# New orders for the five engines of a two-layer kernel, from a planner that lets VectorE and GpSimd take turns by instruction, counts TensorE's halved clock behind a rest, and knows some steps in smaller pieces

## The chip, the cores and the metric

The kernel runs on one core of a Trainium2 chip. The metric is the device time of one execution in microseconds (us). The engines of a core are TensorE (PE, matmuls), VectorE (DVE), ScalarE (ACT), GpSimd (POOL) and SyncE (SP, which here issues most of the DMAs); each works through its own program, and semaphores order them against each other.

## The reference

A hidden state of 4 sequences of 1024 tokens with 128 features passes through two layers. Each normalises and adds an attention and a feed-forward part, both read from the same normalised input:

```python
xn = layernorm(x)
x = x + rwkv6_attention(xn) + moe_per_head(xn)      # layer 1
xn = layernorm(x)
x = x + latent_attention(xn) + looped_moe(xn)       # layer 2
```

`rwkv6_attention` mixes each token with the one before it (five mixtures), makes r, k, v, a decay w and a gate, and runs per head (4 heads, 16 keys, 32 values) the recurrence `o = r·(S + u k v)`, `S = exp(w) S + k v`, then a group norm, a gate and a projection. `moe_per_head` projects, cuts every token into 8 heads of 16 features, and gives each head the weighted sum of the 2 best of 16 experts (16 to 64 with an exact gelu, and back). `latent_attention` goes through a latent of 64 features; 16 heads of 8 share one key and value, with causal softmax over 1024 tokens. `looped_moe` does two rounds of RMS norm, router (2 of 8 experts, weights normalised) and a SwiGLU with 256 hidden features, each added to its input.

## The kernel before

**Layers.** After a normalisation the first layer runs until about 527 us of the span and the second until the end, with a barrier between them (`k.meet`): each engine drains its queue and waits for the four others.

**First layer.** `Recurrence` handles the recurrence in 4 turns of two tiles of 512 tokens, by doubling: `LEVELS` 1, 2, 4, ..., 64. At each level h VectorE updates running products (`level`, L1032: the line L1052 for the part before, L1053 for the part behind, L1054 for the totals; this is the step "factors"), and then scales keys and receptances by them (`vector_scales`, four heads of L1131 and one L1136; steps "scale", it, h, n with n = 0, 1, 2 for heads 0 and 1, heads 2 and 3, and L1136). TensorE multiplies the results (L741, "lev"), VectorE and ScalarE place them ("place", L1074). At the end of a turn comes "qk" (the last level and two products), then "carry", "outs" and the group norm: sums of squares (ScalarE L977, TensorE L846), roots (ScalarE L982), L857, L1199 and gate L1203. The expert part goes through 64 units, each with four up products ("up", TensorE L483), four gelus (ScalarE L529), four down products ("down", TensorE L495), the weighting with the router's shares (VectorE L544 to m_prod and m_both, GpSimd L585 adds them, "pair") and a fold ("fold", L508). `Entry` and `Route` prepare already here the routing for the second layer, for four chunks of 512 tokens in the order `MADE`: GpSimd scales a chunk with three instructions L1372, L1374 and L1376 ("scale", c, 1.0 to 1.2 us each), TensorE turns it (L1425, "zn"), VectorE copies it (L1455, "znc"), TensorE makes the logits (L1431, "elog"), VectorE copies these (L1458, "elogc"). At the end TensorE has a fixed filler of eight matmuls (`busy`, L56).

**Second layer.** `Layer1Start` makes the latent (TensorE L1884, "lat"; its input ax_y is copied by ScalarE L1919, "nc"), queries and keys. The attention has 16 tasks: a first pass over scores for the maxima (TensorE L2807, VectorE L2853), a second one for exponentials (TensorE L2952, ScalarE L2976) and the weighted sums (TensorE L2915), then division (VectorE L3043, L3045) and output. `Experts` runs 96 blocks of 128 gathered token slots in 4 phases: rows and weights are fetched by SP (L3167 and L3155), TensorE makes tokens (L3198, "t"), the products a (L3214) and b (L3230), hidden times weights (L3246, "y_half"), ScalarE copies the result and SP stores it; GpSimd's indirect DMAs scatter (L3108) and gather (L3138), and VectorE adds the gathered results ("combine", L3333 and L3338), followed by the last adds (L3054, L3348).

**The order.** The order of all this is not in the code's control flow. Each engine's part of a class is a generator ("stream"), which before each piece of work yields the planned time of that step; `merge(..., ordered=True)` (L64) emits the stream whose time is least. The times come from a planner, `Plan`: steps have a fixed duration (`takes`), a latency to their dependents (`lag`), needs, PSUM banks that they fill and free, and a flag `port` for VectorE and GpSimd steps that exclude each other at SBUF. `FIRST_ORDERS` and `SECOND_ORDERS` hold one string for each engine, one letter for each step; a letter names the stream whose next step comes. `Plan.run(orders)` only replays these strings: it gives each step a time in the given sequence and assigns the PSUM banks in the order of time. So a program depends on the string for the sequence, and on the replayed times for the banks and the interleaving of streams.

## Time and profile before

| | us |
|---|---|
| median of 3 runs | 1273.62 |
| lowest, highest | 1271.74, 1275.04 |
| the profiled execution's own time | 1275.04 |
| its span in the trace | 1273.7 |
| mean granted TensorE clock in it | 0.976 of full speed |
| TensorE / VectorE / ScalarE / GpSimd busy | 1187.4 / 1048.3 / 881.5 / 488.4 |
| instructions | 28619 |

Positions in the trace are microseconds from the start of the span. A busy engine is one with an instruction under way. The profile's page has the busy times, 40 equal slices of the span and the chain of work that ended last; windows give busy times of a stretch with the number of instructions and the granted clock; a timeline gives the instructions of an engine in order, with the idle time in front and the engine, tile and line that ended it in square brackets. "x4" at the end of a timeline row says that four equal instructions stand in one row. Half clock reads 0.50 where a whole window has it.

### The profile page before, as it was taken

What the parts mean: (1) busy time and instruction counts of PE and PEld (TensorE: products, weight loads), DVE (VectorE), ACT (ScalarE), POOL (GpSimd) and SP (SyncE); (2) the same over time, 40 slices, a digit from 0 to 9 for tenths busy, and PEclk for the clock granted to TensorE, in tenths of its full rate; (3) what the DMA queues carried; (4) which work ended last, traced back from release to release, by engine and by line L of the source; (5) the groups of instructions that cost most, each with busy time, mean ns of one, the idle gap of its engine ahead of it and who ended that gap; (6) DMA issues with size and microseconds to landing.
All of it is one profiled execution on the core that took longest, in us unless ns stands there. A gap on an engine that the chain in (4) does not pass through costs nothing.

```text
span 1273.7 us, 28619 instructions
## 1 busy us (share of the span) xinstructions
PE 1187.4 (93%) x11270; PEld 604.5 (47%) x11270; DVE 1048.3 (82%) x1954; ACT 881.5 (69%) x1243; POOL 488.4 (38%) x446
## 2 busy tenths in 40 slices
PE   6889999999998999798999999998999999999977
PEld 3333433334442324465655555555656555555434
DVE  4699779979999885689979898687987898888734
ACT  3588998988798889262366675665766577666666
POOL 3544344374436664420345503555035550000242
PEclk8799999999999999799999999999999999999988
DMA  7433334323232442347654544545434444224111
GB/s 217 131 129 120 108 96 137 101 74 113 94 126 67 142 140 100 99 127 201 191 172 124 172 115 134 163 133 142 109 118 148 119 116 126 76 74 130 32 34 55
DMA packets 129877, 152.97 MB, mean 120 GB/s; under 512 B 16048, under 2 KB 90800, under 8 KB 129616
## 3 DMA queue, kind: packets, MB, share of 16 engines
q1 hardware_dynamic: 111104, 127.50, 33.3%
q0 software_dynamic: 8192, 16.79, 4.6%
q10 hardware_dynamic: 10448, 6.85, 1.8%
q8 instruction: 90, 1.47, 0.5%
q14 instruction: 43, 0.35, 0.1%
HBM read 109.27 MB, written 41.81 MB: 119 GB/s over the span
## 4 chain that ended last, share of the span: by engine, by line
PE 52%; DVE 13%; ACT 4%; issue 3%; DMA 1%; another core or an unknown queue 1%; SPq 0%; DVEq 0%; ACTq 0%
PE ax_sums L2915 9%; PE second_pair L2952 5%; PE second_pair L2807 5%; PE first_pair L495 3%; PE first_pair L483 3%; PE second_pair L3246 2%; PE second_bank L3230 2%; DVE am_top L2853 2%; PE second_bank L3214 2%; ACT ax_prob L2976 2%; PE second_pair L3230 2%; PE second_pair L3214 2%; PE second_bank L3246 2%; PE second_pair L2929 2%; PE second_pair L2825 2%
## 5 line engine op out<-in xcount | busy, mean ns | idle before, releaser
L2976 ACT ACTIVATE ax_prob<-second_pair 128x1024 f32<-128x1024 f32 (+1 forms) x320 | 291.5, 941 | 128.4 <-PE second_pair L2929 64.9
L529 ACT ACTIVATE m_act_h<-first_pair,const 128x1024 f32<-128x1024 f32 x256 | 273.3, 1115 | 47.9 <-PE first_pair L483 39.3
L2853 DVE TENSOR_REDUCE am_top<-second_pair 128x2 f32<-128x1024 f32 (+1 forms) x192 | 222.4, 1175 | 29.0 <-PE second_pair L2807 11.2
L3138 POOL DMA_INDIRECT m_back<-slot_results,mr_slots x128 | 125.5, 980 | 255.4 <-PE second_pair L2952 154.6
L3108 POOL DMA_INDIRECT slot_tokens<-xn,mr_slots x128 | 125.0, 977 | 238.2 <-PE second_pair L3214 104.1
L2915 PE MATMUL ax_sums<-ax_prob,al_vs 128*32 128x512 f32 (+3 forms) x1536 | 155.9, 500 | 5.6 <-ACT ax_prob L2976 4.0
L483 PE MATMUL first_pair<-m_terms,w1s 96*128 96x512 bf16 x512 | 143.5, 387 | 2.7 <-ACT m_act_h L529 2.1
L495 PE MATMUL first_pair<-m_act_h,const 128*32 128x512 f32 x1024 | 129.0, 607 | 7.5 <-DVE m_both L544 2.6
L585 POOL TENSOR_TENSOR m_both<-m_prod,m_both 128x512 f32<-128x512 f32 x64 | 86.2, 1358 | 108.2 <-DVE m_both L544 108.0
L2952 PE MATMUL second_pair<-al_qs,al_ks 51*128 51x512 bf16 (+3 forms) x768 | 113.9, 333 | 10.5 <-ACT ax_prob L2976 4.5
L2807 PE MATMUL second_pair<-al_ks,al_qs 48*128 48x512 bf16 (+3 forms) x768 | 112.8, 329 | 8.6 <-DVE am_top L2853 2.9
L483 PEld LDWEIGHTS first_pair<-m_terms,w1s 96*128 96x128 bf16 x512 | 38.5, 98 | 119.8 <-issue 60.7
L2853 DVE TENSOR_REDUCE am_later<-second_pair 128x2 f32<-128x768 f32 (+1 forms) x64 | 68.7, 1087 | 19.5 <-PE second_pair L2825 15.4
L2952 PEld LDWEIGHTS second_pair<-al_qs,al_ks 51*128 51x128 bf16 x768 | 33.2, 94 | 83.2 <-issue 34.0
L2807 PEld LDWEIGHTS second_pair<-al_ks,al_qs 48*128 48x128 bf16 x768 | 33.1, 93 | 74.2 <-issue 25.3
L1168 POOL TENSOR_TENSOR rw_mix<-rw_mix,xn 128x512 f32<-128x512 f32 x40 | 48.5, 1227 | 35.9 <-DVE rw_mix L1018 35.2
L2915 PEld LDWEIGHTS ax_sums<-ax_prob,al_vs 128*32 128x32 f32 x1536 | 35.9, 109 | 54.4 <-issue 34.6
L495 PEld LDWEIGHTS first_pair<-m_act_h,const 128*32 128x32 f32 x1024 | 24.9, 109 | 72.2 <-issue 44.5
L3214 PE MATMUL second_pair<-m_tok,m_wt 128*128 128x256 f32 (+1 forms) x204 | 55.3, 361 | 2.1 <-issue 1.0
L544 DVE SCALAR_TENSOR_TENSOR m_prod<-first_pair,const,m_share 128x512 f32<-128x512 f32 x64 | 47.2, 745 | 11.9 <-issue 6.1
L3246 PE MATMUL second_pair<-m_wt,m_hid 128*128 128x128 f32 x360 | 56.1, 280 | 0.5 <-DVE m_hid L3321 0.4
L3230 PE MATMUL second_pair<-m_tok,m_wt 128*128 128x256 f32 (+1 forms) x216 | 53.4, 344 | 1.9 <-ACT m_y L3297 1.9
(402 smaller groups left out, 2556.0 us busy)
## 6 DMA issues: line engine op xcount, KB each, us to landing
m_wt<-in_experts SPq DMA_DIRECT2D x96, 384.0 KB
m_share<-shares SPq DMA_DIRECT2D x128, 256.0 KB
m_rows<-slot_tokens SPq DMA_DIRECT2D x60, 128.0 KB
slot_results<-m_y SPq DMA_DIRECT2D x60, 128.0 KB
stack<-mp_part SPq DMA_DIRECT2D x48, 128.0 KB
m_terms<-stack SPq DMA_DIRECT2D x64, 96.0 KB, 4.2
qstack<-ap_qpart SPq DMA_DIRECT2D x48, 128.0 KB
al_qs<-qstack SPq DMA_DIRECT2D x32, 192.0 KB
```

What stands on the lines that cost most here:

```text
L483: p = E.matmul(banks.bank("up", n, ep)[:, j, :], self.w1s[:, (4 * half + ep) * P:(4 * half + ep + 1) * P], self.terms[:, q % slots, :], st ...
L495: p = E.matmul(banks.bank("down", n, j)[32 * ep:32 * ep + 32, :], self.w("w2", 32 * (4 * half + ep), 32 * (4 * half + ep) + 32), self.act_ ...
L529: A.activation(self.act_h[:, slot, :, :], banks.bank("up", n, ep)[:, :, :], ACT.Gelu, bias=self.w("b1", 4 * half + ep, 4 * half + ep + 1)) ...
L2807: p = E.matmul(banks.bank("max", i, m)[:, x, first:first + n], *self.keys_queries(i, blk, a, x, seg, n), start=a == pairs[0], stop=True, s ...
L2853: V.tensor_reduce(into[:, 2 * a:2 * a + 2, at], tile[:, :, 0:n], AX, ALU.max, negate=True).then_inc(*banks.empties("max", i, m))
L2915: p = E.matmul(self.sums[VW * h:VW * h + VW, off:TILE], self.loads.vs[:, b % 2, blk, :], self.prob[:, g % 3, h, off:TILE], start=blk == 0, ...
L2952: p = E.matmul(tile[:, x, first:first + n], self.loads.ks[rows, b % 2, blk * CH:(blk + 1) * CH], self.loads.qs[rows, i % Q_SLOTS, a, th * ...
L2976: A.activation(dst, src, ACT.Exp, scale=SCALE).then_inc(*banks.empties("sum", i, u))
L3108: G.indirect_dma_start(self.tokens[g], bass.IndirectOffsetOnAxis(ap=self.route.slots[g][second][:, i:i + 1], axis=0), self.entry.zn(GC * g ...
L3138: G.indirect_dma_start(self.back[q % 2][:, n, m, :], None, self.results[ph], bass.IndirectOffsetOnAxis(ap=self.route.slots[g][n][:, c * NC ...
L3214: p = E.matmul(banks.bank("a", ph, b)[:, f * slots:(f + 1) * slots], self.wt[n % 4][:, f * P:(f + 1) * P], self.tok[n % 2][:, 0:slots], st ...
L3246: p = E.matmul(banks.bank("y", ph, b)[:, s * HID:(s + 1) * HID], self.hid[n % 2][:, f * slots + s * CH:f * slots + (s + 1) * CH], self.wt[ ...
```

## The change

Three things are changed; no instruction is added, removed or changed in its shape or operands.

1. **The planner's model.** A TensorE step that starts more than `REST` = 1.6 us after the end of the one before, and every TensorE step that starts within `COLD` = 5.5 us after that start, takes double its duration. And in a replay, of the engines' next steps the one with the earliest start goes first, and with equal starts now the one that was ready first without counting the port (`asked`); before, such a tie went to the engine that stands first in a fixed list, VectorE ahead of GpSimd.
2. **Finer steps.** "factors" (0.77) becomes "before", "behind" and "factors" (0.35, 0.35, 0.16); "scale" becomes one step for each of the four heads (0.29 or 0.4) and one for L1136 (0.36), where two heads were one step before (0.76); "qk" (2.1) becomes "level", "qp" and "qk" (0.8, 0.64, 0.64); GpSimd's scale of the first layer's entry (3.45) becomes three steps "scaled" (1.15 each). In the second layer the scale remains one step.
3. **New strings** in both tables, for all five engines.

The core of the diff (the strings are left out; all 10 are new):

```diff
-    def level(self, it, h):
+    def level(self, it, h, parts=(0, 1, 2)):
...
+            if 0 in parts:
+                V.tensor_tensor(po, po, tt[:, :, 0:1].broadcast_to([P, n, g]), ALU.mult)
+            if 1 in parts:
+                V.tensor_tensor(se, se, tt[:, :, 1:2].broadcast_to([P, n, g]), ALU.mult)
+            if 2 in parts:
+                V.tensor_tensor(self.total[h][:, :].unsqueeze(2), tt[:, :, 0:1], tt[:, :, 1:2], ALU.mult).then_inc(self.levelled, 1)
...
-                    yield FIRST["factors", it, h]
-                    self.level(it, h)
+                    for part, name in enumerate(("before", "behind", "factors")):
+                        yield FIRST[name, it, h]
+                        self.level(it, h, (part,))
...
-                    if x == 2:
-                        yield FIRST["scale", it, h, 1]
+                    if x:
+                        yield FIRST["scale", it, h, x]
...
-            yield FIRST["qk", it]
+            yield FIRST["level", it]
             self.level(it, CH)
+            yield FIRST["qp", it]
...
+            yield FIRST["qk", it]
...
         for c in MADE[:GC]:
-            yield FIRST["scale", c]
-            self.k.pool.wait_ge(loaded, 16)
-            self.scale(c)
+            for part in range(self.SCALES):
+                yield FIRST["scaled", c, part]
+                self.k.pool.wait_ge(loaded, 16)
+                self.scale(c, part)
...
+REST, COLD = 1.6, 5.5
...
+            asked = since
             if port:
                 since = max(since, self.port)
...
-            engine = min(sorted(best, key=ENGINES.index), key=lambda e: min(best[e])[-1] if orders else min(best[e])[0])
+            engine = min(sorted(best, key=ENGINES.index), key=lambda e: min(best[e])[-2:] if orders else min(best[e])[:1])
...
+            if engine == "PE":
+                if start - engine_free.get(engine, 0.0) > REST:
+                    cold = start + COLD
+                if start < cold:
+                    takes *= 2
```

What the strings say at the places that the prediction speaks of, decoded into step names (it is "step", turn, level, part):

```
VectorE near 327 us
before: factors.2.8, invert0.1, znc.2, place.2.2.0, product.36.1, place.2.2.1, elogc.2,
        scale.2.8 (4 heads, L1136), factors.2.16, znc.1
after:  before/behind.2.8, invert0.1, factors.2.8, place.2.2.0, place.2.2.1,
        scale.2.8 (4 heads, L1136), before.2.16, step.6.5, product.36.0, product.36.1, znc.2,
        comb.8, behind.2.16, place.2.4.0, product.37.0, place.2.4.1, elogc.2, factors.2.16, znc.1
GpSimd there
before: shift.6, pair.17.0, pair.17.1, scale.1, scale.3, pair.18.0
after:  pair.17.0, pair.17.1, scaled.1.0, shift.6, scaled.1.1, scaled.1.2, scaled.3.0, scaled.3.1,
        scaled.3.2, pair.18.0
End of the first layer
before: squares (L977) behind gelu.63.3, gm (L846) behind up.63.3
after:  squares behind gelu.63.1, gm ahead of up.63.2
Start of the second layer, SP
before: row.0.0, rest of the constants, row.0.1, row.0.2, weights.0.0
after:  row.0.0, weights.0.0, row.0.1, row.0.2, weights.0.1, weights.0.2, rest of the constants
TensorE there
before: ..., lat.0, lat.1, a.0.0
after:  ..., a.0.0, a2.0.0, lat.0, b.0.0
```

Mean displacement of a step in its engine's sequence, in places: first layer TensorE 1.9, ScalarE 1.5, VectorE 3.8, GpSimd 1.4, SP 1.6; second layer 4.2, 1.9, 1.9, 0.02 and 2.7.

## Rows read from the trace of the kernel before

**Rows 1.** the page: busy time by engine, and the chain that ended last

```profile
PE 1187.4 (93%) x11270; PEld 604.5 (47%) x11270; DVE 1048.3 (82%) x1954; ACT 881.5 (69%) x1243; POOL 488.4 (38%) x446
...
PE 52%; DVE 13%; ACT 4%; issue 3%; DMA 1%; another core or an unknown queue 1%; SPq 0%; DVEq 0%; ACTq 0%
```

**Rows 2.** windows: PE, PEld, DVE, ACT, POOL busy (x), PE clock, DMA share, GB/s

```profile
498.00:527.00 29.00, 24.52 (x183) 11.76 (x179) 10.36 (x16) 12.33 (x17) 12.01 (x12) 0.82 0.13 46
527.00:560.00 33.00, 27.56 (x146) 19.63 (x146) 29.06 (x66) 19.38 (x38) 17.12 (x14) 0.95 0.45 135
...
640.00:1200.00 560.00, 545.94 (x5404) 316.75 (x5403) 473.70 (x814) 368.81 (x598) 173.81 (x180) 1.00 0.43 123
1200.00:1274.00 74.00, 58.90 (x603) 26.85 (x599) 31.24 (x79) 44.93 (x56) 30.45 (x31) 0.89 0.18 48
```

**Rows 3.** windows behind two rests of TensorE, same columns

```profile
339.00:343.00 4.00, 4.00 (x77) 2.32 (x74) 3.59 (x9) 2.19 (x3) 0.59 (x1) 0.57 0.31 117
...
513.00:524.00 11.00, 10.84 (x41) 5.85 (x34) 3.71 (x6) 1.63 (x2) 2.30 (x2) 0.53 0.01 1
```

**Rows 4.** timeline of VectorE, 325 to 345: start, us, work [idle before]

```profile
329.82 4.83 DVE L1131 SCALAR_TENSOR_TENSOR rw_selves<-rw_pre,const,rw_rec 128x256 f32<-128x256 f32 x4
...
335.69 0.68 DVE L1455 COPY rw_hidden<-first_pair 128x512 f32<-128x512 f32 x1
```

**Rows 5.** timeline of GpSimd, 322 to 343

```profile
330.74 1.22 POOL L1372 TENSOR_TENSOR xn<-x,en_moments 128x512 f32<-128x512 f32 x1
```

**Rows 6.** timeline of TensorE, 324 to 345

```profile
327.36 1.07 PE L483 MATMUL first_pair<-m_terms,w1s 96*128 96x512 bf16 x4
...
336.42 1.06 PE L1431 MATMUL first_pair<-const,rw_hidden 128*128 128x8 f32 x8 [1.93 <-DVE rw_hidden L1455]
...
341.92 1.40 PE L483 MATMUL first_pair<-m_terms,w1s 96*128 96x512 bf16 x4
```

**Rows 7.** the scale line L1131, all its instructions: ns min/median/max

```profile
L1131 DVE SCALAR_TENSOR_TENSOR rw_selves<-rw_pre,const,rw_rec x96: 447/480/1512, 68.9 to 482.4; 128x256 f32<-128x256 f32 x96
```

**Rows 8.** groups by form, VectorE, 30 to 527: busy us, mean ns

```profile
L1131 DVE SCALAR_TENSOR_TENSOR rw_selves<-rw_pre,const,rw_rec 128x256 f32<-128x256 f32 x96 | 52.8, 603 | 1.1 <-PE first_pair L741 0.9
```

**Rows 9.** timeline of all engines, 506 to 524

```profile
511.28 0.75 DVE L544 SCALAR_TENSOR_TENSOR m_prod<-first_pair,const,m_share 128x512 f32<-128x512 f32 x1 [2.22 <-PE first_pair L495]
...
512.74 1.42 PE L495 MATMUL first_pair<-m_act_h,const 128*32 128x512 f32 x8 [2.57 <-DVE m_both L544]
...
514.10 3.83 PE L857 MATMUL first_pair<-rw_hidden,const 32*128 32x128 f32 x16
...
517.85 3.78 PE L56 MATMUL first_pair<-shared 128*128 128x256 f32 x8
...
521.57 1.94 PE L508 MATMUL first_pair<-m_both,const 128*32 128x512 f32 x8
```

**Rows 10.** line L529, the gelu and its table loads: ns min/median/max

```profile
L529 ACT ACTIVATE m_act_h<-first_pair,const x256: 1096/1114/1170, 53.1 to 505.6; 128x1024 f32<-128x1024 f32 x128
L529 ACT ACT_TABLE_LOAD  x14: 1283/1283/1283, 51.8 to 439.3; - x14
```

**Rows 11.** timeline of SP, 528 to 537

```profile
530.33 1.22 SPq L3155 DMA_DIRECT2D m_wt<-in_experts  x2
```

**Rows 12.** DMA issues from 528 to 537: KB each, us to landing

```profile
const<-in_const SPq DMA_DIRECT2D x1, 400.0 KB, 4.0
```

**Rows 13.** timeline of TensorE, 528 to 542

```profile
533.20 0.41 PE L3198 MATMUL second_pair<-shared,m_rows 128*128 128x128 f32 x2 [2.73 <-ACT ax_y L1919]
...
536.50 1.38 PE L3214 MATMUL second_pair<-m_tok,m_wt 128*128 128x256 f32 x4
```

**Rows 14.** timeline of TensorE, 1193 to 1198

```profile
1194.69 0.71 PE L3246 MATMUL second_bank<-m_wt,m_hid 128*128 128x128 f32 x4
```

**Rows 15.** timeline of VectorE, 1205 to 1275

```profile
1256.36 1.13 DVE L3333 SCALAR_TENSOR_TENSOR zt<-m_back,mr_share,zt 128x128 f32<-128x128 f32 x4
...
1265.22 0.26 DVE L3043 RECIPROCAL ao_inverse<-second_pair 128x16 f32<-128x16 f32 x1 [6.18 <-PE second_pair L3014]
```

More of the change, by code:

```diff
@@ L1132, in vector_scales @@
                 if h > 1:
-                    yield FIRST["scale", it, h, 2]
+                    yield FIRST["scale", it, h, NH]
                     if h == 2:
@@ L1842, in gpsimd @@
                 self.k.pool.wait_ge(loads.zeroed, 2)
-            self.entry.scale(c)
+            for part in range(self.entry.SCALES):
+                self.entry.scale(c, part)
     def gpsimd_zero(self, loads):
@@ L2431, in plan_levels @@
     for half in range(2):
-        pe("levels", ("lev64", it, half), at, 0.97, ("scale", it, 64, 2), lag=0.3, fills=1, uses=[("lev64", it, half, s) for s in range(2)])
+        pe("levels", ("lev64", it, half), at, 0.97, ("scale", it, 64, NH), lag=0.3, fills=1, uses=[("lev64", it, half, s) for s in range(2)])
         for s in range(2):
```

156 lines of the change are left out of this document (82 added, 74 removed).

## The prediction

> **What bounds the kernel now.** I read the page's first part, the chain of work that ended last, the table of windows, and then the timelines of the places where TensorE stands still. TensorE is busy for 1187.4 of 1273.7 us and makes up 52% of the chain, VectorE 13%, ScalarE 4% [rows 1]. So time can come from three things only: TensorE's idle time (1273.7 − 1187.4 = 86.3 us), matmuls run at half clock, and stretches in which another engine paces it. The windows say where. From 640 to 1200 TensorE is busy 545.94 of 560 us at full clock, so only 14.1 us are open there [rows 2]. Around the seam of the two layers (498 to 560) it idles 4.5 + 5.4 us, and the granted clock is 0.82 and 0.95; in the last 74 us it idles 15.1 at 0.89 [rows 2]. A granted clock of 1.00 is the 2.4 GHz level, 0.5 the 1.2 GHz level. Behind TensorE's rests at 334 and 510 windows of 4 and 11 us show 0.57 and 0.53 [rows 3].
>
> **The change part by part.** No instruction is added or removed and no shape changes, so the sum holds displaced waits and clock alone. Decoding the letters of the tables gives the new sequences; where I say that a step comes earlier or later, it is read from these.
>
> *a. GpSimd's entry scale beside VectorE's scale (327 to 343).* Four scale instructions of L1131 stand as one group of 4.83 us [rows 4], where one of them has a median of 0.48 [rows 7], so 1.92 is work and 2.91 is waiting. Beside them GpSimd runs its three instructions for chunk 3, the first of them 1.22 us [rows 5]: between two VectorE instructions one of GpSimd's gets its turn. The copy for chunk 1 (znc, L1455) is queued behind all of it on VectorE, at 335.69 [rows 4], and TensorE rests 1.93 us for it; then four up products take 1.40 us, where at 327.36 four took 1.07 [rows 6]. The half-clock stretch lies at 339.2 to 342.7, and halving 3.4 us costs 1.7. So the place holds 1.93 + 1.7 = 3.6 us. In the new tables scale.2.8 is ahead of most of scaled.3, GpSimd puts shift.6 between the pieces, and an up product stands ahead of elog.1, but znc.1 remains behind another level's factors. The bounds are 0 and −3.6; I take −2.5, because one turn of GpSimd (1.2 us) will still fall somewhere in front of znc.1.
>
> A rule of the Trainium skill bears on this ("SBUF — State Buffer", section "Who interferes with whom"): VectorE with two SBUF inputs and a GpSimd instruction that reads SBUF exclude each other for the whole instruction, and whichever is issued first has the port. The trace agrees with 4.83 us for four [rows 4]. By that rule the chip takes turns by instruction whatever a step holds, so cutting a step in three by itself changes nothing, and the edit would be worth 0 where its pieces stay adjacent.
>
> *b. The other port turns of the first layer.* The mean of the 96 scale instructions is 603 ns against a median of 480, and 96 × 0.123 = 11.8 us [rows 7, 8]. Less the 2.9 of part a, 8.9 us of VectorE's time are waiting at the port. What of it reaches TensorE lies between VectorE's share of the chain (13% [rows 1], 1.2 us) and the 0.66 of part a (1.93 of 2.91, 5.9 us). Of the seams in formerly joined steps, 6 of 56 between scale pieces, 17 of 40 between factors and 3 of 8 between GpSimd's pieces now have another step in them; the rest stay as they were. The new sequence may also create a collision like that at 329. Bounds −8.9 and +2.9; I take −2.5, some two fifths of 5.9, since most pieces keep their neighbours but the runs as wholes stand elsewhere.
>
> *c. The end of the first layer (506 to 524).* TensorE rests 2.57 us until VectorE's m_both (512.74), and then runs L495, L857, the fixed filler L56 and L508 at half clock [rows 9]: from 514.10 to 523.5 it is the only worker in the path. The 16 small L857, the filler of eight, and L508 take 3.83, 3.78 and 1.94, 9.55 us in all; at the full clock 4.8. So 2.57 + 4.8 = 7.4 us are there at most. The new table moves the squares of the group norm and gm ahead of two gelu steps (before: after gelu.63.3, now after gelu.63.1), each 1.11 us [rows 10], so the norm's chain should be 2.2 us earlier against the expert work, and TensorE has L846 and up.63.2 to do in the other's shadow. But down.63.0, down.63.1, fold.15 and the last products follow one another in the same order as before, and in the rest before 512.74 no engine at all starts anything from 509.6 until VectorE and ScalarE go on at 511.3 (VectorE had idled 2.22 us [rows 9]), which a sequence cannot repair. Bounds 0 and −7.4; I take −3, that is the earlier norm chain (2.2) and a sixth of the clock loss.
>
> *d. The start of the second layer (527 to 560).* SP's queue will issue weights.0.0 as its second entry instead of behind three others, and TensorE puts the first expert product a.0.0 (L3214) ahead of lat.0 (L1884). Before, the weights were issued at 530.33 and the product ran at 536.50, behind both halves of lat; TensorE rests 2.73 us at 533.20 for ax_y [rows 11, 13]. From issue to landing no row of the weights tells, but their neighbour, 400 KB of constants, took 4.0 us [rows 12], and 6.2 from issue to first use is the most; I take 5.1. Issued at the earliest a queue entry after the span's 528.6, at 529.1 to 529.6, they land between 533.1 and 535.3. ScalarE no longer does the softmax with its table load (1.28 us, of the kind in [rows 10]) before nc.0, which brings lat's input forward by as much if nothing else holds it. Bounds: −2 (the rest shrinks by that 1.28, and the clock stays up for some 1.4 us that ran halved) and +4.9 (weights at 535.3 and the product's 1.38 us [rows 13] put lat.0 at 536.7, 3.2 after before, when it followed close behind 533.20, and half of a half-clock stretch of 3.4, as in part a, comes on top). I take 0 between.
>
> *e. The rest of the second layer.* 14.1 us of idle in 560, most of it hand-offs under 0.5 us. TensorE's steps are displaced by 4.2 places on average, with 646 changes of tile shape instead of 633; GpSimd's 368 letters hardly move. Bounds +2 (a new rest like 1.93 [rows 6]) and −5 (a third of 14.1); I take −1.5, a tenth.
>
> *f. The tail.* The last phase's y_half.3.23, at 1194.69 [rows 14], has the gathers behind it. It was 116 TensorE steps from the end and is 106 now, and with (1273.7 − 1194.7) / 116 = 0.68 us for a step it comes 6.8 us later. The last combine starts at 1256.36 with two runs of 1.13, and VectorE's last sums come at 1265.22 after 6.18 us of idling [rows 15]: 1256.36 + 2.2 + 6.8 = 1265.4, so all but 0.2 us of the delay fits into that cover; if it doesn't, the combine's 2.2 us lie in front of the last adds. In the last 74 us TensorE runs at 0.89 and rests 15.1 [rows 2], two of these rests ending in moments where all engines stand. I take +0.5 (0 to +2.2).
>
> Sum: −2.5 − 2.5 − 3 + 0 − 1.5 + 0.5 = −9.0 us against the profiled execution's own 1275.04, that is 1266.0. That execution lies 1.4 above the median of the three (1273.62), so the forecast for a median is 1264.6.
>
> **The rivals.**
> *Bigger gain.* Parts a and c come in full (−3.6 and −7.4), b at −5.9, d, e and f as above: −17.9 from the median, near 1256. For it: the planner now counts the halved clock, whose cost lies exactly in places a, c and the tail. Against: the stand-still of all engines at 509.6 is not in its model, and b's waits are mostly hidden behind TensorE, which is the 52% of the chain [rows 1].
> *No change.* The chip took turns by instruction already (four VectorE instructions, 2.91 us of turns [rows 4]); the finer steps only make the model agree with it, 78 of the 104 seams stay as they were, and each stall removed turns up in front of another step, since the work on VectorE and ScalarE is the same. Time 1273.6. For it: TensorE is busy 97.5% in the longest stretch [rows 2], with nothing to win. This is also what the port rule above would give for the splits.
> *Slower.* At the seam, the product a.0.0 waits for its weights in front of lat.0, and the latents, from which all scores of the attention come, are late. With the middle of the landing, 5.1 us after an issue at 529.6, it starts at 534.7, lat.0 at 536.1: 2.6 us, and 1.7 for the clock, +4.3 with the rest gaining nothing, 1278. It decides if the weights land after 533.5, where lat.0 began, a few tenths behind L3198 [rows 13]. For it: 4.0 us after the earliest issue is 533.1 already. Against: a rest at that place existed before too, and the product's own 1.38 us is moved, not added.
>
> **How the numbers follow.** Forecast 0.40, bigger gain 0.18, no change 0.24, slower 0.18. A difference under 0.3% (3.8 us: 1269.8 to 1277.4) cannot be told from none with this kernel. Forecast and bigger gain are both beyond it: faster 0.58, same 0.24, slower 0.18. The range reaches from 1253 (the bigger gain with a whole further −3 from e, its bound −5) to 1278 (the slower case's centre); the forecast's own range is 1259 to 1269, with b and c at nothing or double their value.
>
> **What would show it.** a: the group of L1131 beside L1372 to L1376 under 3 us, and no window at 0.57 near 339. b: the mean of L1131 under 0.56 us. c: the clock in the last 11 us of the first layer above 0.6, rest before L495 under 2. d: first L3214 ahead of L1884 without a rest over 2.7. e: idle time over the long stretch under 13. f: the last combine within 12 us of the end. The prediction is wrong if TensorE's rests of over 1.5 us are as many and as long as before at other places, if the seam's rest grows, or if bank waits arise that the table of before did not have, because the planner's doubled durations give other banks.

## The result, and the profile after

The changed kernel takes 1286.93 us (median of 4 runs, 1282.08 to 1290.16), the kernel before 1272.68 (4 runs). The ratio is 1.0112, with a 95% interval of 1.007 to 1.0153: slower by some 14 us. The forecast was 1264.6 with a range of 1253 to 1278, so both the sign and the range were wrong.

The page of the changed kernel, with the two lines that answer to [rows 1]:

```profile
span 1286.3 us, 28621 instructions
...
PE 1198.6 (93%) x11270; PEld 610.8 (47%) x11270; DVE 1035.9 (81%) x1954; ACT 878.7 (68%) x1243; POOL 486.9 (38%) x446
...
PE 70%; DVE 13%; ACT 7%; issue 5%; DMA 3%; SPq 1%; POOL 0%; another core or an unknown queue 0%; DVEq 0%; ACTq 0%
```

TensorE is busy for 11.2 us more with the same 11270 matmuls, VectorE for 12.4 us less. TensorE's idle time hardly changed (1286.3 − 1198.6 = 87.7, before 86.3). "issue", time in which an engine waits for nothing that the profile shows, has gone from 3% to 5% of the chain. The windows (columns as in [rows 2]) say where:

```profile
319.00:340.00 21.00, 20.44 (x320) 9.19 (x317) 18.41 (x42) 18.17 (x18) 9.26 (x10) 1.00 0.30 96
430.00:480.00 50.00, 49.36 (x656) 16.35 (x650) 43.85 (x99) 43.55 (x46) 18.59 (x16) 1.00 0.37 118
480.00:530.00 50.00, 39.10 (x303) 16.14 (x300) 20.78 (x37) 24.47 (x31) 20.76 (x20) 0.90 0.18 60
...
640.00:1211.00 571.00, 551.53 (x5410) 318.56 (x5408) 473.31 (x817) 366.10 (x596) 171.94 (x179) 1.00 0.42 122
1211.00:1287.00 76.00, 60.31 (x617) 29.67 (x609) 31.94 (x80) 47.00 (x61) 30.55 (x32) 0.90 0.18 49
```

The place of part a is repaired: from 319 to 340 TensorE idles 0.56 us, at full clock. From 480 to 530 it idles 10.9 us with only 303 matmuls. The long stretch takes 571 us instead of 560, and TensorE idles 19.5 us in it instead of 14.1 [rows 2]. In the last 76 us it idles 15.7, as before (15.1).

The scale line of VectorE, in the view of [rows 8] (30 to 515 us of the span):

```profile
L1136 DVE SCALAR_TENSOR_TENSOR rw_selves<-rw_pre,const,rw_rec 128x256 f32<-128x256 f32 x96 | 41.4, 481 | 0.2
```

Its mean is now 481 ns, where it was 603: the 11.8 us of port waits of this line are all gone. I followed equal steps through both traces (a step's own start, for instance a gelu's): the changed first layer is 5.8 us ahead at gelu 59, and 9.9 us behind at gelu 63. Between these two stands TensorE's timeline of the changed kernel:

```profile
487.07 1.16 PE L768 MATMUL first_pair<-rw_selves,rw_low 64*32 64x128 f32 x30
488.67 0.38 PE L768 MATMUL first_pair<-rw_selves,rw_low 64*32 64x128 f32 x2 [0.44 <-issue]
490.07 0.16 PE L654 MATMUL first_pair<-bf_ident 64*64 64x1 bf16 x1 [1.02 <-issue]
...
502.90 0.43 PE L829 MATMUL first_pair<-rw_full,rw_val 128*32 128x128 f32 x5 [0.22 <-issue]
503.62 0.43 PE L829 MATMUL first_pair<-rw_full,rw_val 128*32 128x128 f32 x5 [0.28 <-issue]
504.35 0.41 PE L829 MATMUL first_pair<-rw_full,rw_val 128*32 128x128 f32 x4 [0.29 <-issue]
```

These are steps of many small matmuls (lev32, lev64, outs of the last turn), which no semaphore stops; the last of them come in clumps of four or five with a pause after each. Meanwhile VectorE and ScalarE wait for TensorE, so this is not a wait handed on. The pauses marked issue come to 5.6 us here. Behind them TensorE also runs at half clock, where eight matmuls of L495 take 1.93 us instead of 1.07:

```profile
493.00:500.00 7.00, 6.35 (x23) 1.90 (x22) 0.75 (x1) 4.89 (x9) 1.20 (x2) 0.51 0.05 18
506.00:510.00 4.00, 3.40 (x6) 1.05 (x5) 0.00 (x0) 0.00 (x0) 2.83 (x3) 0.59 0.15 49
```

Up to the seam most of the loss is made up again: TensorE starts the second layer at 528.5 in the changed kernel and at 527.3 in the one before, 1.2 us apart. From there to the end the two traces take 757.7 and 746.4 us, 11.3 apart.

So two losses and one gain are to be explained: a starved TensorE at the end of the first layer, a longer second layer, and a first layer that is ahead until then.

### The profile page after: what moved, and what is told of

Same layout as the page of the kernel before. It is cut to its first block, busy times and chain, and to the rows that moved or that the text cites. A ratio compares the mean times of both kernels' runs of the same rounds, so it can differ in the third digit from the quotient of the medians.

```text
span 1286.3 us, 28621 instructions
## 1 busy us (share of the span) xinstructions
PE 1198.6 (93%) x11270; PEld 610.8 (47%) x11270; DVE 1035.9 (81%) x1954; ACT 878.7 (68%) x1243; POOL 486.9 (38%) x446
## 4 chain that ended last, share of the span: by engine, by line
PE 70%; DVE 13%; ACT 7%; issue 5%; DMA 3%; SPq 1%; POOL 0%; another core or an unknown queue 0%; DVEq 0%; ACTq 0%
PE ax_sums L2941 10%; PE first_pair L495 7%; PE first_pair L483 7%; PE second_pair L2978 6%; PE second_pair L2833 5%; ACT m_act_h L529 3%; PE second_pair L3240 3%; PE second_pair L3272 3%; PE second_bank L3256 2%; PE second_pair L3256 2%; PE second_bank L3240 2%; PE second_bank L3272 2%; ACT ax_prob L3002 2%; PE second_pair L2955 2%; DVE am_top L2879 2%
## 5 line engine op out<-in xcount | busy, mean ns | idle before, releaser
L529 ACT ACTIVATE m_act_h<-first_pair,const 128x1024 f32<-128x1024 f32 x256 | 273.4, 1115 | 42.2 <-PE first_pair L483 35.9
L585 POOL TENSOR_TENSOR m_both<-m_prod,m_both 128x512 f32<-128x512 f32 x64 | 86.3, 1358 | 125.6 <-DVE m_both L544 125.4
L495 PE MATMUL first_pair<-m_act_h,const 128*32 128x512 f32 x1024 | 131.1, 614 | 3.0 <-DVE m_prod L544 1.3
L2978 PE MATMUL second_pair<-al_qs,al_ks 51*128 51x512 bf16 (+3 forms) x768 | 113.1, 332 | 11.3 <-issue 5.6
L1175 POOL TENSOR_TENSOR rw_mix<-rw_mix,xn 128x512 f32<-128x512 f32 x40 | 50.5, 1275 | 43.9 <-DVE rw_mix L1018 43.8
L544 DVE SCALAR_TENSOR_TENSOR m_both<-first_pair,const,m_share 128x512 f32<-128x512 f32 x64 | 47.1, 741 | 16.1 <-PE first_pair L495 12.7
L3240 PE MATMUL second_pair<-m_tok,m_wt 128*128 128x256 f32 (+1 forms) x220 | 58.2, 354 | 1.7 <-issue 0.7
L3301 ACT ACTIVATE m_tok<-second_pair 128x256 f32<-128x256 f32 (+1 forms) x71 | 24.4, 349 | 51.5 <-PE second_pair L3224 39.4
L3256 PE MATMUL second_pair<-m_tok,m_wt 128*128 128x256 f32 (+1 forms) x220 | 57.8, 354 | 0.5 <-ACT m_y L3323 0.4
L495 PEld LDWEIGHTS first_pair<-m_act_h,const 128*32 128x32 f32 x1024 | 25.6, 110 | 66.9 <-issue 45.4
```

What stands on the lines that cost most here:

```text
L495: p = E.matmul(banks.bank("down", n, j)[32 * ep:32 * ep + 32, :], self.w("w2", 32 * (4 * half + ep), 32 * (4 * half + ep) + 32), self.act_ ...
L529: A.activation(self.act_h[:, slot, :, :], banks.bank("up", n, ep)[:, :, :], ACT.Gelu, bias=self.w("b1", 4 * half + ep, 4 * half + ep + 1)) ...
L2978: p = E.matmul(tile[:, x, first:first + n], self.loads.ks[rows, b % 2, blk * CH:(blk + 1) * CH], self.loads.qs[rows, i % Q_SLOTS, a, th * ...
L3240: p = E.matmul(banks.bank("a", ph, b)[:, f * slots:(f + 1) * slots], self.wt[n % 4][:, f * P:(f + 1) * P], self.tok[n % 2][:, 0:slots], st ...
L3256: p = E.matmul(banks.bank("b", ph, b)[:, f * slots:(f + 1) * slots], self.wt[n % 4][:, MF + f * P:MF + (f + 1) * P], self.tok[n % 2][:, 0: ...
```

## The experiments

The chips used differ: the kernel before takes 1241 to 1243 us on some (called the faster kind here) and 1272 to 1277 on others, the slower kind, to which the result above belongs. Each chip served for one batch of runs only, so it is not shown whether the difference stays with a chip. Each kernel is compared with the kernel before on its own chip; differences below are (ratio − 1) × the time of before there, with the interval in brackets.

| kernel | before there | ratio (95%) | us |
|---|---|---|---|
| again (changed kernel, one run) | 1241.08 | | +14.3 |
| first_new | 1241.08 | 0.9953 (0.9934 to 0.9972) | −5.8 (−8.2 to −3.5) |
| second_new | 1241.08 | 1.0106 (1.0081 to 1.0131) | +13.2 (+10.1 to +16.3) |
| planner_only | 1241.08 | 1.0252 (1.0221 to 1.0284) | +31.3 (+27.4 to +35.2) |
| before_again (one run) | 1242.65 | | +8.3 |
| tail_new | 1242.65 | 1.001 (0.9994 to 1.0027) | +1.2 (−0.7 to +3.4) |
| start_new | 1242.65 | 1.0008 (0.9991 to 1.0024) | +1.0 (−1.1 to +3.0) |
| tail_fix | 1242.65 | 1.0079 (1.0057 to 1.01) | +9.8 (+7.1 to +12.4) |
| half_new | 1277.27 | 1.0032 (1.0009 to 1.0054) | +4.1 (+1.1 to +6.9) |
| later_new | 1277.27 | 1.004 (1.0021 to 1.0059) | +5.1 (+2.7 to +7.5) |
| fine_old | 1277.27 | 1.0337 (1.0304 to 1.0369) | +43.0 (+38.8 to +47.1) |
| first_new_2 | 1271.97 | 1.0055 (1.0033 to 1.0077) | +7.0 (+4.2 to +9.8) |
| first_new_3 | 1242.51 | 0.9924 (0.9898 to 0.995) | −9.4 (−12.7 to −6.2) |
| early_new | 1242.51 | 0.9968 (0.995 to 0.9986) | −4.0 (−6.2 to −1.7) |
| early_new_2 | 1276.03 | 0.9943 (0.9918 to 0.9968) | −7.3 (−10.5 to −4.1) |
| early_old | 1242.51 | 1.0016 (0.9992 to 1.0039) | +2.0 (−1.0 to +4.8) |
| late_old | 1242.51 | 1.0004 (0.9986 to 1.0021) | +0.5 (−1.7 to +2.6) |
| late_old_2 | 1276.03 | 1.0041 (1.0017 to 1.0066) | +5.2 (+2.2 to +8.4) |

### Which layer

**again** is the changed kernel, unaltered.

> The changed kernel unaltered, one more execution with a trace. Its first trace shows the first layer 6 to 10 us ahead of the kernel before until unit 61, and then a stretch from 488 to 512 in which TensorE starves (gaps marked issue, 3.6 us, and matmul groups that take longer than their like), so that the seam is reached 1.5 us late. Theory A (the starving belongs to the program): the same stretch shows again, time 1283 to 1290. Theory B (a chance event of that execution): it is absent here or somewhere else, and the first layer ends 10 to 15 us earlier than in the first trace; the time is then under 1280, unless such an event falls in another place.

1255.35 us, where before takes 1241.08. The starved stretch is not there: TensorE's gaps with "issue" come to 1.2 us in the whole execution, where the first trace had 17.4. Theory B seemed to hold; it fell later. The loss against before was 14.3 us all the same. It comes from one execution, though, and the one execution of before_again below lies 8.3 us above the median of its own kernel.

**first_new** is the changed kernel with planner, strings and banks of before in the second layer.

```diff
 def second_layer():
-    p = Plan(2 * PAIRED + 1, PAIRED, patience=PATIENCE2, loath=LOATH2)
+    p = OldPlan(2 * PAIRED + 1, PAIRED, patience=PATIENCE2, loath=LOATH2)
```

> The first layer of the changed kernel, the second layer of the kernel before (its order and banks). Theory A (the loss is in the second layer's new order, and the first layer's gain is real but eaten by one event): 1263 to 1270, faster than before by 3 to 9 us. Theory B (the first layer's end starves in the new order in every execution): 1274 to 1278, slower by 1 to 5 us.

−5.8 us: Theory A. **second_new** is its mirror image: the kernel before, with the new planner and `SECOND_ORDERS` in the second layer.

> The first layer of the kernel before, the second layer of the changed one (order and banks). The replayed plan of the second layer ends at 725.8 against 720.6 before, 5.3 us later; the two traces show 10 to 11 us from the seam on. Theory A (the new second order is the loss): 1278 to 1285. Theory B (the loss is at the seam or in the first layer): 1271 to 1275.

+13.2 us, Theory A. On this chip the second layer alone more than accounts for the loss (−5.8 + 13.2 = +7.4 against a single +14.3, the one run of "again"). The mirror image was not run on the slower kind. There first_new_2, half_new and later_new, all below, give 7.0 + 4.1 + 5.1 = 16.2 us, inside the interval of the result (8.9 to 19.5).

**before_again** is the kernel before, for a trace of the faster kind.

> The kernel before, unaltered, for a trace from the chip on which the experiments run (there it takes 1241 us, not 1273). Both theories expect 1238 to 1247. If the second layer takes about 720 us from the seam to the end, as in the run with the new first layer alone (719.6), and the first about 517, then the split of the loss can be read from traces of one chip.

A single run of 1250.99, above the range and above all 23 runs of before on that chip (1245.59 at most), so a difference of some 8 us between single runs shows nothing. TensorE enters the second layer at 521.6. From 523.9, its fourth group of matmuls there, which is the seam in these counts, to the end it takes 725.6 us. In four other traces of this kind whose second layer is the old one, in whole or for the most part (first_new, planner_only, tail_new, start_new), it takes 719.6 to 723.8; with the new one it takes 730.9 (second_new) and 740.0 (again).

### The second layer: start, middle and tail

The old and new strings can be cut into each other where all engines' prefixes hold the same steps. Each of the next kernels is the kernel before with such a mixed `SECOND_ORDERS`; the planned end is that of the replay.

**start_new**: new to 72 us of the plan, old from there.

> The kernel before; only the first part of the second layer's strings (to about 72 us of the plan) is the changed one; plan 721.2. With the new rule for ties the planner gives the old start 8.4 us more than the new one. Theory A (that price is of the model alone: the chip lets VectorE in between GpSimd's three instructions of an entry scale): within 2 us of before, plan says +0.6. Theory B (the price is real): faster by 5 to 9 us. Theory C, of the prediction's slower case (expert weights late in front of lat.0): slower by 3 to 5.

+1.0: Theory A. The price that the new planner puts on the old start (a second-layer entry scale of 3.4 us holds the port as one step, and VectorE waits for all of it) does not exist on the chip. Replayed, it is 8.7 us, not 8.4: the old strings end at 729.3 in the new planner and at 720.6 in the old one. With the entry scales taken off the port the new planner says 720.5.

**half_new** and **later_new** split the new strings at 300 us of the plan.

> The kernel before; the second layer's strings are the changed ones up to about 300 us of the plan and the old ones from there; plan 722.7 (+2.1). Theory A (the loss follows the plan's length, 1 to 2 us on the chip for each us of the plan): slower by 2 to 4 us. Theory B (the loss lies in the second half and the tail alone): within 1.5 us.

> The kernel before; the second layer's strings are the old ones up to about 300 us of the plan and the changed ones from there; plan 723.9 (+3.4), tail included. Theory A (plan's length plus the tail's 4 to 7 us that the plan does not show): slower by 8 to 11 us. Theory B (the loss is mainly in the first half): slower by less than 4.

+4.1 and +5.1, where the plan says +2.1 and +3.4. Theory A held for the first, at its upper edge. The second lies between its two theories: the tail that was expected on top was missing. **tail_new** has only the new tail.

> The kernel before; only the last part of the second layer's strings (from about 666 us of the plan) is the changed one. The replayed plan ends at 720.6, as before (720.6). Theory A (VectorE's combines 3.0 and 3.1 wait for gathers in front of inverse.5.3, and TensorE for ao_scaled behind them, with a half-clock stretch after): slower by 4 to 7 us. Theory B (the plan's end tells the chip's: no tail loss): within 2 us.

+1.2: Theory A falls, and with it my account of the tail as a loss by itself. VectorE's timeline of second_new shows what the tail does behind the new middle:

```profile
1207.48 1.12 DVE L3446 SCALAR_TENSOR_TENSOR zt<-m_back,mr_share,zt 128x128 f32<-128x128 f32 x4
...
1213.67 1.14 DVE L3446 SCALAR_TENSOR_TENSOR zt<-m_back,mr_share,zt 128x128 f32<-128x128 f32 x4 [4.02 <-DMA m_back<-slot_results,mr_slots]
...
1216.06 0.29 DVE L3158 TENSOR_TENSOR ao_scaled<-second_bank,ao_inverse 128x128 f32<-128x128 f32 x1
```

and TensorE's:

```profile
1216.40 0.66 PE L3137 MATMUL second_bank<-shared,ao_scaled 128*128 128x128 f32 x4 [3.78 <-DVE ao_scaled L3158]
```

combine.3.1 waits 4.02 us for a gather, inverse.5.3 is queued behind it, and TensorE rests 3.78 us for ao_scaled. In tail_new the gathers had started early enough: combine.3.1 runs 27 us after y_half.3.23, in second_new VectorE reached it after 22. **tail_fix** moves inverse.5.3 in front in second_new:

```diff
-parts.15 combine.3.0 combine.3.1 inverse.5.3 combine.3.2
+parts.15 inverse.5.3 combine.3.0 combine.3.1 combine.3.2
```

> First layer of before, the whole second layer of the changed kernel, with one step moved in VectorE's string: inverse.5.3 two places forward, ahead of combine.3.0 and combine.3.1; the banks and the plan's end (725.8) stay. The same without the move took 1.0106 of before (+13 to +16 us). Theory A (this step behind the combines is the tail's loss): 4 to 7 us come back, 1247 to 1252 where before is 1241. Theory B (the loss is spread over the second layer): no change, 1253 to 1258.

+9.8 against +13.2. The intervals overlap, so the times alone do not show the 3.4 us. In the trace combine.3.1 still waits (4.33 us), but TensorE rests nowhere for ao_scaled, and from y_half.3.23 to VectorE's last instruction it takes 56.2 us instead of 60.7. The spans differ by 1.0 us only (1249.6 and 1250.5), because y_half.3.23 itself comes 3.5 us later in tail_fix. So the rest and its cause are shown, and that it is worth 3 to 5 us is not. In before_again the same stretch takes 60.8 us, with ten steps more in it.

The remaining loss is spread over the second layer, and part of it is TensorE's own time: TensorE is busy there for 698.8, 703.5 and 709.4 us in second_new, tail_fix and again, and for 695.4 to 698.5 in the nine other traces of this kind. It idles 28.4 to 34.4 us in these three and 26.2 to 29.5 in the nine. The weighted sums, all 1536 of them, in the groups of first_new (old order) and of second_new (new):

```profile
L3044 PE MATMUL ax_sums<-ax_prob,al_vs 128*32 128x512 f32 (+3 forms) x1536 | 153.0, 494 | 0.1
```

```profile
L3028 PE MATMUL ax_sums<-ax_prob,al_vs 128*32 128x512 f32 (+3 forms) x1536 | 157.1, 499 | 0.1
```

They take 157.1 us instead of 153.0. The other traces of this kind with the old order have 152.9 to 153.9; tail_fix has 156.3 and again 156.9. Two things come together. In second_new 16 of these matmuls ran at half clock, in first_new none. And the new order has them in 144 unbroken rows of 10.7 on average, the old one in 137 of 11.2; the sum of their durations is 4.88 times their busy time in the new order and 4.96 times in the old. Where the half clock is equal (eight matmuls each in tail_fix and before_again), the smaller overlap goes with 2.4 us (156.3 against 153.9).

The planner's new rules have no part in this loss: in the old planner the new `SECOND_ORDERS` give every step the same time, and every use the same bank, as in the new one. Whether they cost by the sequence or by the banks that come with it (807 of 1151 are not those of before) no run separates.

### Banks

**planner_only** is the kernel before with the class `Plan` and the constants of the change, and nothing else.

> The kernel before with the changed planner alone (rest and cold doubling, ties by readiness), its own strings and its coarse steps. The sequences of all engines stay; 167 of 655 PSUM banks in the first layer and 13 of 1151 in the second are assigned differently. Theory A (banks do not matter, only sequences do): no change, 1271 to 1276. Theory B (the banks of the new replay make new waits): slower by 4 or more.

+31.3: Theory B, and by much more than it asked. **fine_old** has the fine steps too; the second layer is that of before.

> Planner and fine steps of the change in the first layer, but the first layer's old sequence spelled out in them; the second layer is that of before. The sequences of all engines are those of before; 200 of 655 banks differ, and the replayed first layer ends at 514.0 instead of 460.2. Theory A (banks given by a timeline in which GpSimd holds VectorE up make real waits, as with the planner alone, +34 us): slower by 20 to 40 us. Theory B (the coarse steps were what made the planner alone slow): within 4 us of before.

+43.0: Theory A. In both, each engine does the same instructions in the same order as before, in the traces too; what differs is the PSUM bank of 167 and of 200 of the first layer's 655 uses (and of 13 of the second's 1151 in planner_only), with the waits that go with them. TensorE's waits, longest first, in planner_only from 30 to 549:

```profile
PE first_pair L483 <- ACT m_act_h L529: 20.2, 29, 1.3
PE first_pair L238 <- ACTq L60: 4.4, 1, 4.4
```

and the same wait in before_again, from 30 to 521:

```profile
PE first_pair L483 <- ACT m_act_h L529: 1.2, 3, 0.5
```

The up products wait 20.2 us in 29 places for a gelu that still reads their bank, 19 of the 31 us; in fine_old they wait 28.5 us in 34 places. The new planner replays the old first layer to 514 us where the old one says 460: it believes GpSimd holds VectorE up, thinks some banks free earlier than others, and hands out banks for a run that doesn't happen. Of the two new rules it is the one for ties: with the old tie rule in its place, and the doubling kept, the replay ends at 460.2 again and all 655 banks are the old ones. With the doubling alone switched off it still ends at 504.3, with 153 banks changed. With the new strings the first layer ends at 461.1 in the replay, and most of this harm is gone: the same wait is 6.5 us in 9 places in the changed kernel, and 2.1 us in 5 in the one before.

### Scatters and gathers beside TensorE

**first_new_2** is first_new on another chip.

> The version with the changed first layer and the second layer of before once more, since it is the only one faster than both kernels (0.9953, 0.9934 to 0.9972, on a chip where before takes 1241 us). Theory A (the first layer's new order is worth 4 to 8 us whatever the chip): ratio 0.994 to 0.997 again. Theory B (a chance of that set of runs): 0.998 to 1.002.

1.0055, and neither theory: slower, beyond the interval. Before takes 1272 us here, and the starved stretch is back at the same steps as in the first trace of the change:

```profile
487.34 0.38 PE L768 MATMUL first_pair<-rw_selves,rw_low 64*32 64x128 f32 x2 [0.54 <-issue]
488.78 1.08 PE L783 MATMUL first_pair<-rw_selves,rw_low 64*64 64x256 f32 x3 [0.94 <-issue]
...
501.47 0.44 PE L829 MATMUL first_pair<-rw_full,rw_val 128*32 128x128 f32 x5 [0.30 <-issue]
502.20 0.43 PE L829 MATMUL first_pair<-rw_full,rw_val 128*32 128x128 f32 x5 [0.28 <-issue]
```

So the stretch belongs to the program and the kind of chip: both traces of this first layer on the slower kind have it, and all three on the faster kind lack it. GpSimd's timeline of the same run shows what runs beside it:

```profile
483.88 0.96 POOL L3237 DMA_INDIRECT slot_tokens<-xn,mr_slots  x1 [0.31 <-issue]
485.14 0.96 POOL L3237 DMA_INDIRECT slot_tokens<-xn,mr_slots  x1 [0.30 <-issue]
486.41 0.96 POOL L3237 DMA_INDIRECT slot_tokens<-xn,mr_slots  x1 [0.30 <-issue]
487.67 0.96 POOL L3237 DMA_INDIRECT slot_tokens<-xn,mr_slots  x1 [0.30 <-issue]
```

The new order has scatters 17 to 24 beside lev32 and lev64 and 25 to 31 beside outs; the old one, in the trace of before, has two just ahead of lev32, one beside lev64 and two beside outs. To test it, scatters alone were moved on GpSimd, with banks and all other sequences kept:

```diff
+SCATTERS_AFTER = {("mix", 3, 4, 0): 3, ("mix", 3, 4, 1): 3, ("pair", 27, 1): 6, ("pair", 28, 1): 6}
+    for step, many in SCATTERS_AFTER.items():
+        for i in range(many):
+            FIRST["scatter", n] = FIRST[step] + 0.001 * (i + 1)
```

This is **early_new** (on first_new); **early_old** and **late_old** do the like to the kernel before, forward and back. **first_new_3** is first_new as a companion.

> The new first layer with the second layer of before, once more, as the companion of the next kernel on the same chip. By the two earlier results: about 0.995 of before if before takes some 1241 us on this chip, about 1.005 if some 1272 us. Theory A and B expect the same here.

> The same kernel; on GpSimd alone the scatters 14 to 31 are moved forward into its idle time (behind mix.3.4.0, mix.3.4.1, pair.27.1 and pair.28.1), so that none is left beside lev32, lev64 and outs of the last turn; banks and all other sequences stay. Theory A (the indirect DMAs beside steps of many small matmuls starve TensorE on chips of the slower kind): on such a chip 8 to 13 us faster than its companion, TensorE's issue gaps near 487 to 505 gone; on a chip of the faster kind within 2 us. Theory B (the starving has another cause, of the steps themselves): within 2 us of the companion on either kind, gaps still there.

> The kernel before with its scatters 14 to 31 moved forward into GpSimd's idle time (behind mix.3.4.1, pair.26.1, pair.27.1 and pair.28.1); all else is before. Theory A: on a chip of the slower kind 3 to 6 us faster than before (its trace lost some 5 us there against the faster kind from 495 to the seam), within 2 us on the faster kind. Theory B: within 2 us on both.

> The kernel before with its scatters 17 to 31 moved back: six behind pair.29.1, three behind pair.30.0 and six behind pair.30.1, which puts them beside lev64, carried and outs as in the new order; all else is before. Theory A: on a chip of the slower kind 4 to 10 us slower than before, with issue gaps on TensorE near lev64; within 2 us on the faster kind. Theory B: within 2 us on both.

The chip was of the faster kind. The new first layer has −9.4, early_new −4.0, early_old +2.0, late_old +0.5: moving the scatters gains nothing here, and in early_new it costs 5 us, more than the 2 that were expected. Two of them were run again, on a chip of the slower kind:

> As early_new. If before takes about 1272 us on this chip (slower kind): theory A, 0.993 to 0.999 of before and no issue gaps on TensorE in lev64 of the last turn, where the unaltered new first layer had 1.0055 and gaps; theory B (not the scatters): 1.003 to 1.008 with gaps. If before takes 1241 us: 0.995 to 0.999 as before, which tells nothing new.

> As late_old. If before takes about 1272 us on this chip: theory A, 1.003 to 1.008 of before, with issue gaps on TensorE beside the scatters in lev64 and outs; theory B: 0.998 to 1.002. If before takes 1241 us: 0.999 to 1.002 again.

By the times Theory A on both. late_old is the cleaner test: +5.2 on the chip of its own before, with nothing but scatters moved. The early order's −7.3 stands against +7.0 of the unaltered one, which was measured on another chip and not run here beside it; the first layers of the two traces end 1.3 us apart only (525.1 and 526.4). TensorE in late_old_2 has gaps where GpSimd's scatters now are:

```profile
497.40 0.27 PE L768 MATMUL first_pair<-rw_selves,rw_low 64*32 64x128 f32 x1 [1.07 <-issue]
498.84 0.38 PE L483 MATMUL first_pair<-m_terms,w1s 96*128 96x512 bf16 x1 [0.85 <-issue]
```

and on GpSimd:

```profile
496.49 1.28 POOL L3120 DMA_INDIRECT slot_tokens<-xn,mr_slots  x1 [0.30 <-issue]
498.07 0.96 POOL L3120 DMA_INDIRECT slot_tokens<-xn,mr_slots  x1 [0.30 <-issue]
```

They are not at the place that the theory named. They stand in lev32 and in an up product, which is not a small matmul; the 16 matmuls of L495 behind them take 3.06 us instead of 1.93 at full clock. lev64 has no gap, and outs has the 0.25 us that before has too (0.26). Followed by equal instructions, late_old_2 is 2.4 us behind the trace of before at 485 and 6.2 at 505.

In early_new_2 the gaps moved with the scatters to an up product (0.93 us at 466) and an earlier level's step, and are shorter there (2.4 us from 460 to 510, 3.5 in first_new_2):

```profile
473.71 0.71 PE L741 MATMUL first_pair<-rw_selves,rw_low 64*32 64x64 f32 x46
475.06 0.32 PE L741 MATMUL first_pair<-rw_selves,rw_low 64*32 64x64 f32 x4 [0.64 <-issue]
475.81 0.34 PE L741 MATMUL first_pair<-rw_selves,rw_low 64*32 64x64 f32 x4 [0.43 <-issue]
```

All traces together say the same. In the eight of the slower kind 103 of TensorE's 128 gaps marked issue (55.0 of 66.5 us) overlap an indirect DMA on GpSimd, a scatter or a gather, though these fill only 19 to 20% of the span. In the twelve of the faster kind there are at most two such gaps each, 1.2 us at most, and none lies beside an indirect DMA. The gathers count as well. In the changed kernel's last 75 us five gaps, each beside a gather, come to 6.6 us (before: 1.8). The longest:

```profile
1249.43 0.94 POOL L3164 DMA_INDIRECT m_back<-slot_results,mr_slots  x1 [0.30 <-issue]
...
1250.80 0.50 PE L2978 MATMUL second_pair<-al_qs,al_ks 51*128 51x384 bf16 x2 [2.28 <-issue]
```

early_new is also the one version that is faster than the kernel before on both kinds of chip (0.9968 and 0.9943).

## Why the prediction was wrong

The result was taken on the slower kind. There I had −8.0 us for the first layer (a, b, c), and it is +7.0 by first_new_2 (the two first traces have +1.2 at the seam). I had −1.0 for the second (d, e, f), and it is +4.1 and +5.1 for its halves (+11.3 in the first traces), +13.2 on the faster kind. The steps that failed are e, which bounded a new order by the idle time that stood there, and c, which left out GpSimd's scatters.

**Part a (−2.5).** Right in its place. The four scales that took 4.83 us take 1.63 to 1.65 in first_new, and no rest of 1.9 us and no half clock is left from 319 to 340. The expected turn of GpSimd in front of znc.1 did come, on other instructions. In the changed kernel the second product of level 16 ("behind") takes 1.05 us where it takes 0.42 alone, and the totals behind it 0.55 instead of 0.18:

```profile
324.56 1.05 DVE L1056 TENSOR_TENSOR rw_suf<-rw_suf,rw_total 128x256 f32<-128x256 f32 x1
...
328.30 0.55 DVE L1058 TENSOR_TENSOR rw_total<-rw_total 128x32 f32<-128x32 f32 x1
```

TensorE had other work by then and did not rest. Between gelu 36 and gelu 39 (314 to 339 in before) the lead over the old order grows by some 4 us (5.1 to 9.1 in the first traces, 4.7 to 8.8 in again against before_again, 2.1 to 6.1 in first_new against second_new). By gelu 51 1.5 to 4.1 us of it are given back.

**Part b (−2.5, at most −8.9).** The mechanism was right and the count of 26 open seams misleading. The new sequence keeps scales and GpSimd's instructions apart nearly everywhere: the mean of the line fell to 481 ns, its whole 11.8 us. What of this reached TensorE no run measures by itself. The lead of 2.1 to 5.1 us that stands ahead of a's place is the nearest to it.

**Part c (−3).** Wrong in what decides there. I looked at the group norm's chain and the clock. On the slower kind that much was right: the changed kernel runs L857, the filler and L508 at full clock (2.27, 1.99 and 1.07 us instead of 3.83, 3.78 and 1.94 [rows 9]), 4.2 us less. But I never looked at GpSimd's scatters in this stretch, because they cost GpSimd nothing new. On a chip of the slower kind TensorE has its gaps beside them, and the stretch lost 16 us between gelu 59 and 63 in the first trace, of which 8.7 are made up by the seam. a, b and c together are −5.8 and −9.4 on the faster kind (I had −8.0), and +7.0 on the slower one. That the faster kind agrees is partly luck, since what c prices is hardly there: in its eight traces with the old first layer the rest before the last L495 is 0.94 us instead of 2.57, and in six of them L857 and the filler run at full clock already.

**Part d (0).** Right: start_new is +1.0, inside −2 to +4.9. The slower rival, named with its place, did not happen: in the changed kernel a.0.0 runs at 534.3 ahead of lat.0 at 536.0, without a rest of over 0.9 us there.

**Part e (−1.5, bounds −5 to +2).** The step that failed most. The second layer's new order is +13.2 us, of which start and tail by themselves account for 2.2; the rest, about 11, is more than five times e's upper bound, or about four times if tail_fix's 3.4 are taken off. I had bounded it by TensorE's idle time, as if a new order could only give or take waits of the kind that stood there. It can also make the plan itself longer and the matmuls overlap less. That it is longer can be read off without a chip: replayed, the second layer ends at 725.8 instead of 720.6. For the mixed kernels plan and chip rank alike: +0.1, +0.6, +2.1, +3.4 and +5.3 in the plan, and +1.2, +1.0, +4.1, +5.1 and +13.2 us on the chip, the first two within noise and the third and fourth from the slower kind. It is no rule: the first layer's plan is 0.9 us longer too (461.1 against 460.2), and on the faster kind it is the faster one. The new second strings look better only to the new planner, in which the old ones end at 729.3, and the 8.7 us on top of 720.6 are the unsplit entry scale, which start_new shows to be worth nothing.

**Part f (+0.5, at most +2.2).** Right for the tail alone (tail_new +1.2). The failing step is that I held the delay of y_half against the last combine only, which did not even come nearer to the end (17.0 us in front of it, before 17.3). The one that matters is combine.3.1, because inverse.5.3 is behind it on VectorE and TensorE behind that. I had decoded that sequence and not asked who is queued behind the waiting step.

**The rivals.** None of them is what happened. "No change" had one true half: the finer steps and the tie rule do nothing by themselves on the chip's port. But I costed the planner's change at nothing beyond that, with one clause about banks at the very end; planner_only and fine_old show that banks from a false replay are worth 31 and 43 us, more than everything else in this case. The change escapes most of it by its new strings. The port rule of the Trainium skill ("SBUF — State Buffer", section "Who interferes with whom") also held in a way that I did not use: the chip excludes by instruction, so a planner that lets a step of three instructions hold the port as one, as the second layer's entry scale still does, is wrong by 8.7 us in its plan. Two numbers of the working were slips without weight: the forecast's own range, with b and c at nothing or double, is 1259 to 1270, and GpSimd's string for the second layer has 229 letters.

What stays open: the second layer's 11 us are split only in part (2 to 4 in the weighted sums, 3 to 5 in the tail's combine behind the new middle); why TensorE has no work beside a scatter is not shown, only that moving scatters moves the gaps; whether the kernel before would gain on the slower kind from moving its own scatters was not tried there (early_old ran on the faster kind alone); and no run moves the 32 gathers at the end, though that is where the traces of the slower kind lose most (before: from 8 us behind before_again at 1192 to 24 at 1268).

## What to carry to other kernels

Where an order comes from a planner, replay old and new strings in both planners before believing either, and ask whether the price that the search avoided exists on the chip. An order decides more than waits: PSUM banks that are handed out by a replayed clock carry every error of that clock into real waits. And when a step moves, look at what it lies beside on the other engines, also where it costs its own engine nothing, and at who is queued behind each step that waits for a DMA.

## What the runs showed of the hardware

The same kernel takes 1241 to 1243 us on some chips and 1272 to 1277 on others, at a mean granted clock of 0.986 on the first and 0.977 on the second. The difference is not spread evenly. In traces of the kernel before from either kind, the offset stays within 1 us from 190 to 495, then grows by 5 us to the seam. In the second layer it falls to 1 us and rises slowly to 8 at 1192, and it grows by another 16 us in the last 80 us, beside the last gathers. TensorE's gaps marked issue come to 5.3 us on the slower kind and 0.7 on the faster, and 103 of 128 of them on the slower kind overlap an indirect DMA. An order that is better by 0.8% on the one kind can be worse by 0.6% on the other.
